# A graph network's layer stage: TensorE's 100 units as a loop of two, with two fixed places for marks and source features, and VectorE's six passes of 320 as three of 640

## The reference

```
g   = segment_sum(h[src] * edge_weight, dst)      # over 200,000 edges
g   = l2_normalize(g)                             # lift layers only
out = concat([h, g]) @ W + b                      # 64 -> 32
h   = l2_normalize(out)   or   tanh(out)          # lift / proj
```

## Time and the profile before

| what | value |
|---|---|
| runs of the kernel before, median (lowest to highest of 3) | 12,940.66 us (12,935.49 to 12,972.4) |
| profiled execution, first to last instruction | 11,187.8 us |
| profiled execution's own time around its span | not given by the profile |
| median of the runs less the span | 1,752.9 us |
| PE busy, PEld busy | 7,977.6 us (71%), 5,606.9 us (50%) |
| DVE busy | 9,110.1 us (81%) |
| ACT busy, POOL busy | 3,152.1 us (28%), 4,719.6 us (42%) |
| mean granted clock of TensorE | 0.804 |
| units of the 12 layers (first transpose to last) | 2,817.1 to 7,624.5 us |

### The profile page before, as it was taken

One profiled execution on the slowest core, in us unless ns is written; L12 is line 12 of the kernel. 1 busy time (PEld: TensorE's weight loads), 2 busy tenths in 40 slices (PEclk: granted clock), 3 DMA queues, 4 the chain that ended last, 5 costly groups with the idle time before them and its releaser, 6 DMA issues.

```text
span 11187.8 us, 339090 instructions
## 1 busy us (share of the span) xinstructions
PE 7977.6 (71%) x127894; PEld 5606.9 (50%) x127895; DVE 9110.1 (81%) x18642; ACT 3152.1 (28%) x7975; POOL 4719.6 (42%) x5783
## 2 busy tenths in 40 slices
PE   2555555400777877877877878786889988888994
PEld 2444444300666766766766767674444444444442
DVE  8777777658877877877877877778999999999995
ACT  0111111048222222222222222222444444444441
POOL 3777777610311311321221221232665656666661
PEclk9999999975988988988988988997665666566555
DMA  4111111147645655744745755662111111111111
GB/s 174 26 26 25 25 25 25 27 168 249 200 150 152 205 152 151 211 151 150 216 150 152 211 168 161 182 186 77 36 36 35 34 36 36 36 35 35 36 34 19
DMA packets 719340, 1175.84 MB, mean 105 GB/s; under 512 B 155346, under 2 KB 350241, under 8 KB 715001
## 3 DMA queue, kind: packets, MB, share of 16 engines
q1 hardware_dynamic: 435480, 1024.95, 28.9%
q0 software_dynamic: 146832, 67.20, 5.1%
q10 hardware_dynamic: 136012, 67.95, 2.4%
HBM read 1019.27 MB, written 140.22 MB: 104 GB/s over the span
## 4 chain that ended last, share of the span: by engine, by line
PE 41%; DVE 18%; issue 16%; ACT 3%; POOL 1%; DVEq 1%; DMA 1%; ACTq 0%; POOLq 0%; SPq 0%
PE psum L1959 10%; PE psum L1927 10%; PE psum L1942 6%; PE psum L2069 6%; PE psum L2050 3%; DVE space L1476 2%; DVE space L1475 2%; DVE space L1442 2%; PE psum L2034 2%; PE psum L2004 2%; DVE space L1480 2%; ACT space L1590 2%; DVE space L1487 1%; PE psum L2019 1%; ACT space L1595 1%
## 5 line engine op out<-in xcount | busy, mean ns | idle before, releaser
L714 POOL TENSOR_TENSOR claim_out<-claim_in 128x1 f32<-128x1 f32 x1199 | 309.9, 258 | 4943.4 <-DMA table<-space 2405.5
L789 POOL DMA_INDIRECT space<-feature_table,space x2000 | 1943.1, 972 | 612.0 <-issue 611.6
L2050 PE MATMUL psum<-w_mix,space 64*128 64x448 f32 x4144 | 1755.8, 942 | 0.0
L1622 ACT ACTIVATE space<-psum 128x375 f32<-128x375 f32 x2400 | 937.9, 435 | 2866.9 <-PE psum L1927 2862.6
L725 POOL DMA_INDIRECT slots<-space x1568 | 1507.0, 961 | 466.1 <-issue 412.8
L1141 DVE TENSOR_TENSOR space<-psum,space 128x320 f32<-128x320 f32 x2400 | 1065.7, 485 | 727.6 <-PE psum L1942 702.8
L1927 PE MATMUL psum<-space 128*32 128x125 fp8e4 x72000 | 1344.0, 223 | 227.5 <-issue 226.1
L1959 PE MATMUL psum<-space 128*128 128x96 bf16 x24000 | 1287.9, 206 | 217.8 <-issue 163.1
L1927 PEld LDWEIGHTS psum<-space 128*32 128x32 bf16 x72000 | 1077.4, 97 | 484.2 <-issue 474.0
L1959 PEld LDWEIGHTS psum<-space 128*128 128x128 fp8e4 x24000 | 1099.4, 96 | 375.6 <-issue 258.4
L1147 DVE TENSOR_TENSOR space<-space 128x320 f32<-128x320 f32 x2400 | 1059.5, 482 | 2.7 <-issue 2.7
(11 more groups left out here) (275 smaller groups left out, 11948.6 us busy)
## 6 DMA issues: line engine op xcount, KB each, us to landing
space<-marks SPq DMA_DIRECT2D x2400, 320.0 KB
marks<-space SPq DMA_DIRECT2D x100, 640.0 KB, 3.1
space<-distances ACTq DMA_DIRECT2D x200, 320.0 KB
space<-block_ids SPq DMA_DIRECT2D x198, 200.0 KB
slots<-space SPq DMA_DIRECT2D x82, 448.0 KB, 9.1
space<-feature_table,space POOLq DMA_INDIRECT x2072, 2.4
space<-src_rows SPq DMA_DIRECT2D x102, 320.0 KB, 4.0
slots<-space POOLq DMA_INDIRECT x1608, 2.1
```

Of the source, the lines that this page charges most:

```text
L789: g.indirect_dma_start(out=gathered_rows[:, half, t, :], out_offset=None, in_=feature_table, in_offset=bass.IndirectOffsetOnAxis(ap=row_in ...
L1622: a.activation(to[:, s0:s1, :, :], pair_picked[:, bank, 0:(s1 - s0) * PICK_COLS].rearrange("p (k c r) -> p k c r", k=s1 - s0, r=CAP), ACT.Copy
L2050: last = mm(radial[:, 2 * ring + odd, 0:MIX_S + MIX_V], hidden[odd * HIDDEN:(odd + 1) * HIDDEN, slot, upper * LANES:(upper + 1) * LANES], ...
```

## The change

- TensorE's code of a layer becomes: a start for the first units, then a loop over the 5 chunks, and inside it a loop of 10 turns (9 in the last chunk) of two units, then the last two units. The number of turns is loaded from the new tile `chunk_turns`. The order within a turn stays turn_slots, gather, add_unit, but the clearing now stands at the head of a chunk's loop, before turn_slots, and the last add_unit of a chunk behind turn_slots and gather of the units that follow.
- For this, what a unit reads must lie at fixed addresses. The marks have two places (`PLACES`) instead of five. SyncE loads picks for unit n+2 when gather(n) is done and places for n+2 when add_unit(n) is done. The source features of a unit (5 x 3 x 32 elements in every partition) are copied by ScalarE from `parts` into `unit_parts` (two places, where the ring's last places were), one unit ahead of use.
- `add_unit` begins with one matmul of a single column of zeros.
- TensorE runs 48 matmuls of one column at its start and 62 ahead of the convolution (`fill`).
- VectorE's `weigh_unit` makes three passes of 640 elements instead of six of 320. Each pass waits for the one before it.
- ScalarE begins the first two copies when the first quarter of h is split (`parts_started`), and waits for all stores of marks before the layers.

```diff
@@ SyncE
-                    sp.wait_ge(unit_added, layer * UNITS + j * STEPS + q + 1)
-                    for half, loaded in enumerate((picks_loaded, places_loaded)):
-                        sp.dma_start(ring_words[:, q % RING, words], ...).then_inc(loaded[q % RING], 16)
+                with sp.Fori(0, UNITS // PLACES - 2, 1) as i:
+                    for q in range(PLACES):
+                        sp.wait_ge(pair_gathered, layer * (2 * UNITS) + i * (2 * PLACES) + 2 * (q + PLACES) + 2)
+                        load_picks(sp.snap(i * PLACES + q + 2 * PLACES, min_val=0, max_val=UNITS - 1), q)
+                        sp.wait_ge(unit_added, layer * UNITS + i * PLACES + q + RING + 1)
+                        load_places(sp.snap(i * PLACES + q + PLACES, min_val=0, max_val=UNITS - 1), q)
@@ VectorE, weigh_unit
-                for k, half in enumerate(halves):
-                    v.tensor_tensor(row[:, half, :], slots_of_unit[:, half, :], ..., ALU.mult).then_inc(weighed, 1)
-                for k, half in enumerate(halves):
-                    dve.wait_ge(weighed, 2 * n + k + 1 + 2)
-                    v.tensor_tensor(left[:, half, :], row[:, half, :], tops[0][:, half, :], ALU.subtract
-                                    ).then_inc(left_split, 1)
-                for k, half in enumerate(halves):
-                    dve.wait_ge(left_split, 2 * n + k + 1)
-                    v.tensor_tensor(least[:, half, :], left[:, half, :], tops[1][:, half, :], ALU.subtract
-                                    ).then_inc(least_split, 1)
+                v.tensor_tensor(row, slots_of_unit, ..., ALU.mult).then_inc(weighed, 2)
+                dve.wait_ge(weighed, 2 * n + 2 + 2)
+                v.tensor_tensor(left, row, tops[0], ALU.subtract).then_inc(left_split, 1)
+                dve.wait_ge(left_split, n + 1)
+                v.tensor_tensor(least, left, tops[1], ALU.subtract).then_inc(least_split, 2)
@@ ScalarE
+                    def copy_sources(q):
+                        return a.activation(unit_parts[:, q % PLACES, :, :, :],
+                                            parts[:, q * SRC_PER_TILE:(q + 1) * SRC_PER_TILE, :, :], ACT.Copy)
+                    act.wait_ge(parts_started, layer + 1)
+                    for q in range(2):
+                        copy_sources(q).then_inc(sources_copied, 1)
+                    act.wait_ge(parts_ready, layer + 1)
                     with act.Fori(0, CHUNKS, 1) as j:
                         for q in range(STEPS):
...
+                            copy_sources((q + 2) % STEPS).then_inc(sources_copied, 1)
@@ TensorE
+            def await_unit(layer, turn, o):
+                pe.wait_ge(picks_loaded[o % PLACES], 16 * turn + 16 * (o // PLACES) + 16)
+                pe.wait_ge(sources_copied, 2 * layer + PLACES * turn + o + 1)
-                                          parts[:, q * SRC_PER_TILE + s, c, :], cells[:, :, g, CAP * s:CAP * (s + 1)],
+                                          unit_parts[:, place, s, c, :], cells[:, :, g, CAP * s:CAP * (s + 1)],
...
+            def add_unit(turn, o):
+                pe.wait_ge(places_loaded[o % PLACES], 16 * turn + 16)
+                pe.wait_ge(least_split, 2 * PLACES * turn + 2 * o + 2)
+                mm(unit_sums[:, 0, 0:1], zeros_bf[:, 0:LANES], zeros_bf[:, 0:1], start=False, stop=True,
+                   skip_group_check=True)
...
-                for j in range(CHUNKS):
-                    add_chunk(layer, j, j + 1 < CHUNKS)
+                with pe.Fori(0, CHUNKS, 1) as j:
+                    clear_unit_sums(layer * CHUNKS + j)
+                    turns = pe.value_load(chunk_turns[0:1, bass.ds(j, 1)], min_val=CHUNK_TURNS - 1, max_val=CHUNK_TURNS)
+                    with pe.Fori(0, turns, 1) as m:
+                        turn = layer * layer_turns + j * CHUNK_TURNS + m
+                        for o in range(PLACES):
+                            await_unit(layer, turn, o + 2)
+                            turn_slots(turn, o + 1)
+                            gather(o + 2)
+                            add_unit(turn, o)
```

More of the change, by code:

```diff
@@ L97, in build_gnn @@
     UNIT_COLS = UNIT_TILES * LANES
-    RING = 5
-    assert STEPS % RING == 0 and UNITS % 2 == 0
+    RING, RING_WORDS = 5, 2 * UNIT_COLS // 4
+    PLACES = 2
+    LAYER_FILL, CONV_FILL = 48, 62
+    assert STEPS % PLACES == 0 and PLACES < RING
+    CHUNK_TURNS = STEPS // PLACES
+    SOURCE_WORDS = SRC_PER_TILE * 3 * D // 2
+    assert PLACES * SOURCE_WORDS <= RING_WORDS
     PICK_BANKS = ((0, 3), (3, 5))
@@ L1134, in weigh_unit @@
                 buf = q % 2
-                halves = [slice(k * HALF_TILES, (k + 1) * HALF_TILES) for k in range(2)]
                 row, left, least = (message_parts[:, buf, :, c, :] for c in range(PARTS))
@@ L1608, in _ @@
             a.activation(stat2[:, :], stat2[:, :], ACT.Sqrt).then_inc(deviation_ready, 1)
+            for place in range(MADE_RING):
+                act.wait_ge(marks_stored[place], 16 * (UNITS // MADE_RING))
             for lift, first, layers in ((True, 0, LIFTS), (False, LIFTS, PROJS)):
@@ L1823, in _, with fill @@
             mm = nc.tensor.matmul
-            pe.wait_ge(bf_ready, 2)
+            def fill(products):
+                for _ in range(products):
+                    mm(psum[:, 8 * BANK - 1:8 * BANK], zeros_bf[:, 0:LANES], zeros_bf[:, 0:1], start=True, stop=True)
+            pe.wait_ge(bf_ready, 4)
+            pe.wait_ge(cleared, 1)
+            fill(LAYER_FILL)
+            pe.wait_ge(bf_ready, 4)
             pe.wait_ge(cleared, 1)
@@ new lines, in _ @@
+                await_unit(layer, layer * layer_turns, 1)
+                turn_slots(layer * layer_turns, 0)
+                gather(1)
+                with pe.Fori(0, CHUNKS, 1) as j:
[8 more added lines that the diff above has]
+                            add_unit(turn, o)
@@ L1989, in _ @@
+                last_turn = layer * layer_turns + layer_turns - 1
+                for o in range(PLACES):
+                    if o + 2 < PLACES:
+                        await_unit(layer, last_turn, o + 2)
+                    if o + 1 < PLACES:
+                        turn_slots(last_turn, o + 1)
+                    if o + 2 < PLACES:
+                        gather(o + 2)
+                    add_unit(last_turn, o)
                 turns = pe.value_load(spill_turns[0:1, 0:1], min_val=1, max_val=MAX_SPILL_TURNS)
@@ L2038, in _ @@
                 pe.wait_ge(biased, layer * OUTS + OUTS)
+            fill(CONV_FILL)
             pe.wait_ge(weights_spread, 16 * 3)
```

97 lines of the change are left out of this document (44 added, 53 removed).

## The result

The changed kernel takes 13,032.33 us at the median of 6 runs (13,023.72 to 13,053.59), the kernel before 12,948.67 us (12,916.40 to 12,972.40, 6 runs). The ratio is 1.0067, with a 95% interval of 1.0053 to 1.0081: slower, by 84 us. The forecast was 12,670.

What follows compares the result with a forecast made beforehand. It took TensorE, slightly slower than VectorE and stalled by instruction fetches, as the bound; -389 - 150 + 180 + 58 + 0 + 30 = -271 us from a median of 12,940.66 gave 12,670 us, range 12,430 to 12,930.

Steps and rivals of the forecast that it cites:

- The sum's frame: Whole kernel: profiled span 11,187.8 us against a median of 12,940.66; the 1,753 us between were taken as a constant.
- The code no longer fetched: TensorE's layer units: the loop stays in the engine, so fetch stalls go, -389 us, and what follows from them, -150.
- all 204 us without a name: Layers' units: slow time with no one cause, such as engines out of step after stalls; bounds 0 and -204, taken -150.
- Loop control: End of each TensorE loop turn: branch, register step and waits expose 0.3 us, 600 turns, +180 us (0 to +480).
- the marks: Wait ahead of turn_slots with two places: loads land in 3.3 us and hide in the mean, +30 us (0 to +300).
- the extra matmul: Start of add_unit on TensorE: one more matmul per unit, 0.048 us each, 1200 times, +58 us (0 to +58).
- mark loads become the bound: Rival, ahead of turn_slots: landing above 4.1 us makes the kernel slower; at 4.5 us, +240, 13,180 us; chance 0.12.
- Chunk ends: VectorE's weigh, join, clear chain at 48 chunk ends stays the same, -1 to +1 us each: 0.
- VectorE's three passes: VectorE's weigh_unit: 2.45 us a unit against 2.41 before, covered by TensorE's 2.52 or more: cost 0.
- ScalarE's copy: ScalarE's copy of 480 elements per unit: about 0.6 us, needed more than one unit later: cost 0.
- fill (0): TensorE's 110 tiny filling matmuls: cost 0.
- control: Rival, end of loop turns: 0.75 us of a turn exposed instead of 0.3, +270, same time, 12,940 us; chance 0.10.

Runs made afterwards that it cites:

- experiments 5 and 6: GpSimd's 864 indirect transfers of spilled rows replaced by memsets, in the kernel before (12,451.72 us, ratio 0.9667) and in the changed kernel (12,387.06 us, 0.9617).
- experiments 9 and 10: Changed kernel without the spilled rows' transfers: with half of each unit's marks loaded, 12,221.02 us (0.9501); with four places and a four-unit loop, 12,200.57 us (0.9489).
- experiment 11: Changed kernel with the clearing behind a chunk's first gather and four places in a loop of four units, all transfers in: 12,728.42 us, ratio 0.9903.
- Experiment 8: Changed kernel with each chunk's first turn written out ahead of the loop and the clearing behind its first gather: 12,802.09 us, ratio 0.9920.
- Experiments 2 to 4: Changed kernel without fill matmuls, ratio 1.0067; kernel before with three VectorE passes of 640, 1.0003; changed kernel with six passes of 320, 1.0073.
- the second profile: The kernel before, unchanged, profiled once more: span 12,920.9 us, median of runs 12,897.51 us, ratio 1.0004.

## Why the prediction was wrong

Three steps failed. The frame took 1,753 us for a constant that lies in no view. The gain from the fetches, -389 and -150, was priced without the standstill beside GpSimd's transfers: the pace of the units in the kernel as timed came to (0.7 + 0.7 - 3.3) x 12 = -23 us (early, mid and late units), where the sum had -271. And the chunk ends stood at 0 and cost 118 us. A layer's transposes span 347 us (443.9 less 96.6), where 290 were forecast.

**The sum's frame, the first wrong step.** "The 1,753 us between are in no view; I take them as a constant" was false. Every execution whose own time I have ends within 2 us of its span. The one profiled first has no own time on record; by its rows it lacked the standstills, and that is all that shows it to have been shorter. A frame in which 1,753 of 12,941 us are in no view should have cost the forecast its narrow range. The rows of that profile show GpSimd's indirect transfers beside a TensorE that runs on, and each of the twelve later profiles shows the other kind wherever the transfers are in.

**The code no longer fetched (-389, and -150 of what follows).** The mechanism was right: 138 packets, add_unit's issue time 2 us. The size was wrong, because in 72 of 100 units the time is set by something that the prediction didn't have: the 1.0 us standstill. Early units went from 3.487 to 3.498 us. That the fetches hide in the standstill is shown by experiments 5 and 6: take it away and the same edit gains 0.106 us a unit. Even then the term was too large. The prediction had 3.02 us a unit as the pace of before; without the transfers it is 2.88 early and 2.97 late. The pace of after was given as 2.745 and is 2.77. But 2.745 doesn't follow from the sum of -271: it takes all 204 us without a name for gone, where the sum takes 150; by the sum it is 2.79 us a unit and 294 us a layer. So the gain in pace is 61 x 0.106 + 4 x 0.09 + 20 x 0.211 = 11 us a layer, 133 in all, where -271 stood. On the Trainium skill's rule ("Runtime: NRT & Kernel Launch", section "Instruction fetch mechanics", a taken branch out of a two-page window forces a fetch): no run here shows a loop stall by it, not with two units nor with four. The same section gives TensorE 128 KiB for instructions, far more than two of its pages. By an estimate at 64 bytes an instruction the two loops are 24 and 48 KB and fit, while a layer written out is 1,100 KB and doesn't; the trace agrees with that figure, by 138 and 198 packets against 906.

**Loop control (+180) and the marks (+30).** Their sum with the extra matmul's 58 was 268 us, 0.22 a unit; measured is 2.77 - 2.52 = 0.25. That the totals are so close is luck, for the split was wrong. The marks' landing is 0.15 us a unit (experiments 9 and 10), which is 1200 x 0.15 = 180 us and not 30. The landing time itself was right, 3.3 us; what failed is that the load "hides in the mean". Control has 0.15 us a turn where 0.3 stood, 600 x 0.15 = 90 us and not 180, and the extra matmul 0.02 a unit, 24 us and not 58. The rival "mark loads become the bound" had the right place and too high a price: in 28 units of a layer it costs some 50 us (28 x 0.15 x 12), and in the other 72 it hides in the standstill. In experiment 11 four places take 0.19 us off the late units and 0.01 off the early ones.

**Chunk ends (0, bounds -48 to +48): wrong, and the largest cost.** The text says "VectorE's chain (weigh, join, clear) is the same; its two waits become one". That is true and beside the point. What counts is what TensorE does during VectorE's join. Before, it turned and gathered the next unit; after, both stand behind the clearing, which stands behind the join. Measured +9.8 us a layer with the transfers and +8.2 without, 118 and 98 us in all. Experiment 8, which moves the clearing back and writes out a chunk's first turn for it, took the ratio from 1.0067 to 0.9920. The prediction's front part describes the moved clearing, and the step asked about VectorE's queue alone.

**VectorE's three passes (0), ScalarE's copy (0), fill (0): right.** A pass takes 824 to 826 ns (forecast 815), the copy 602 (forecast 600). Experiments 2 to 4 show no effect of passes or fill. Of turn_slots' idle time 14.2 us are put down to ScalarE's copy in the changed kernel and 45.5 without the transfers, but 0.2 when the marks come early, so no cost of its own is shown.

**The rivals.** What came true on the slower side was none of mine: not a slow load, not control, but an order of work on TensorE that lost its overlap, on top of a gain that was hidden.

## What to carry to other kernels

Compare a profile's span with its own execution's time, and with the timed runs, before reading anything else: where they differ by more than a few microseconds, as here by 1,753, the profile's idle times may not be those that a change will meet. When code becomes a loop, list what each engine did during every wait of the old order, and ask whether the new order still has it there. A stall that is removed gains nothing as long as a longer one covers it, so look for the engine that stops the others before pricing the stalls.

## What the runs showed of the hardware

- While GpSimd issues an indirect transfer (0.97 us), TensorE's matmuls of 32 columns stand still for about as long: 1.98 us for a gather that takes 0.97. With plain transfers of 0.55 us they don't. Leaving the 864 out saves 3.3% of this kernel. Why the first profiled execution has the same instructions side by side without a standstill stays open. One thing in its page tells it from all twelve later ones: it has a time from issue to landing for the indirect transfers, and they have none, in any kernel. First the first profile's row, then the second's:

```profile
slots<-space POOLq DMA_INDIRECT x1608, 2.1
```

```profile
slots<-space POOLq DMA_INDIRECT x1608
```

  What that says of the transfers' signals no run shows.
- The stages with many such transfers are the ones that are longer in the second profile: the later stage's loop turns in 81.3 us (39 turns from 8,643.3 to 11,813.2), and in 63.7 by the earlier trace rows, with 2,000 transfers beside it. The granted clock there was a little lower too (0.56 against 0.61), so these rows alone don't say how much is the transfers'; in the sort it is 1.00 in both. In the sort a VectorE copy of eight columns waits 3.37 us for a matmul that started 4 us earlier, while three of these transfers are issued. The profile of the changed kernel calls what it waited for "remote":

```profile
1012.61 0.17 PE L1917 MATMUL psum<-space,ones_bf 128*128 128x8 bf16 x1
...
1012.84 0.96 POOL L746 DMA_INDIRECT slots<-space  x1 [0.30 <-issue]
...
1014.10 0.96 POOL L746 DMA_INDIRECT slots<-space  x1 [0.30 <-issue]
...
1015.37 0.96 POOL L746 DMA_INDIRECT slots<-space  x1 [0.30 <-issue]
1016.56 0.17 DVE L1007 COPY space<-psum 128x8 f32<-128x8 f32 x1 [3.37 <-remote]
```

  In the first profile the same copy never waits in the sort. That these are the same effect is argued from the rows; no run took the transfers of those stages away.
- A loop of four units on TensorE, twice as long as the changed kernel's, ran without being fetched anew in each turn (198 packets against 138). The 60 more are 5 a layer, one a chunk.
